# Transposed one-hots by a broadcast load, expansions between the steps of the scan chain, and one load of eight wait counts

## The reference

```python
ZU = einsum('nd,kdr->knr', Z, U)               # K = 4 heads of R = 16: 64 numbers per node
logits = (ZU[:, src] * ZU[:, dst]).sum(-1) / sqrt(R)
exp_l  = exp(logits - segment_max(logits, dst)[:, dst])
alpha  = exp_l / (segment_sum(exp_l, dst)[:, dst] + 1e-16)
agg    = segment_sum(alpha[..., None] * ZU[:, src], dst)
```

## Time and profile before

| | before |
|---|---|
| median of 3 runs | 3706.7 us |
| the profiled execution, its own time | 3677.74 us |
| its span (first to last instruction) | 3675.2 us |
| busy: PE, DVE, POOL, ACT | 54%, 52%, 47%, 32% |
| share of the 16 DMA engines: SP's queue, POOL's queue | 15.4%, 9.8% |
| granted TensorE clock, mean | 0.577 of full speed |

### The profile page before, as it was taken

One profiled execution on the slowest core, in us unless ns is written; L12 is line 12 of the kernel. 1 busy time (PEld: TensorE's weight loads), 2 busy tenths in 40 slices (PEclk: granted clock), 3 DMA queues, 4 the chain that ended last, 5 costly groups with the idle time before them and its releaser, 6 DMA issues. The chain is left out here.

```text
span 3675.2 us, 61713 instructions
## 1 busy us (share of the span) xinstructions
PE 1971.2 (54%) x15251; PEld 1490.8 (41%) x15252; DVE 1919.5 (52%) x5864; ACT 1168.6 (32%) x3040; POOL 1728.5 (47%) x1832
## 2 busy tenths in 40 slices
PE   9345545454545445454545455464545454567776
PEld 9233333343434334343424243343433333444666
DVE  4444646454545546454545455464545454666477
ACT  1112323222232323322232233233232322334477
POOL 1544454445444444554544544445544444252662
PEclk7555555555555555555555555555555555577798
DMA  6212222121212212121212112121212121285343
GB/s 205 52 32 46 47 44 46 42 46 42 48 41 47 46 41 48 42 49 40 47 39 48 42 44 48 41 50 41 48 40 45 41 49 39 58 274 179 112 140 107
DMA packets 406593, 232.96 MB, mean 63 GB/s; under 512 B 284096, under 2 KB 371434, under 8 KB 406506
## 3 DMA queue, kind: packets, MB, share of 16 engines
q1 hardware_dynamic: 346666, 154.11, 15.4%
q0 software_dynamic: 59840, 77.87, 9.8%
HBM read 134.80 MB, written 42.55 MB: 48 GB/s over the span
## 5 line engine op out<-in xcount | busy, mean ns | idle before, releaser
L576 POOL DMA_INDIRECT arena<-z_table,sslot x1563 | 1492.0, 955 | 1646.2 <-SPq L418 1114.0
L1347 PE MATMUL bank<-arena 128*128 x4992 | 613.8, 222 | 637.7 <-issue 585.8
L1347 PEld LDWEIGHTS bank<-arena 128*128 128x128 bf16 x4992 | 457.5, 105 | 789.5 <-issue 697.0
L1584 ACT ACTIVATE arena<-bank 128x272 f32<-128x272 f32 x416 | 269.8, 661 | 1574.8 <-remote 970.4
L902 DVE TENSOR_TENSOR xin<-arena,bank 128x512 f32<-128x512 f32 x208 | 143.1, 688 | 1044.3 <-remote 588.2
L1561 ACT ACTIVATE acc<-xTb 128x68 f32 x1600 | 384.6, 312 | 306.6 <-issue 296.0
L1364 PE MATMUL bank<-xto,arena 128*128 128x68 bf16 x3328 | 321.6, 246 | 147.5 <-issue 147.4
L1335 PE MATMUL bank<-ident_b,arena 128*128 128x128 bf16 x1664 | 214.8, 310 | 339.4 <-remote 205.3
L1364 PE MATMUL bank<-arena 128*128 128x68 bf16 x1664 | 296.9, 243 | 120.2 <-issue 90.5
L1364 PEld LDWEIGHTS bank<-xto,arena 128*128 128x128 bf16 x3328 | 281.5, 132 | 166.9 <-issue 166.9
L1335 PEld LDWEIGHTS bank<-ident_b,arena 128*128 128x128 bf16 x1664 | 160.4, 141 | 399.6 <-remote 200.2
(11 more groups left out here) (264 smaller groups left out, 2543.6 us busy)
## 6 DMA issues: line engine op xcount, KB each, us to landing
arena<-arena SPq DMA_DIRECT2D x1660, 32.0 KB
arena<-z_table,sslot POOLq DMA_INDIRECT x1563
dspace<-in_xT SPq DMA_DIRECT2D x49, 256.0 KB
xmz_table<-agn SPq DMA_DIRECT2D x49, 256.0 KB
xmz_table<-arena SPq DMA_DIRECT2D x14, 896.0 KB
arena<-in_x SPq DMA_DIRECT2D x13, 896.0 KB, 11.4
out<-arena SPq DMA_DIRECT2D x12, 896.0 KB
xin<-in_xT SPq DMA_DIRECT2D x8, 896.0 KB
```

The source lines that it names most:

```text
L576: pool.indirect_dma_start(ring[:, e % RING, :], None, z_table, bass.IndirectOffsetOnAxis(ap=sslot[:, e:e + 1], axis=0)).then_inc(tiles_in[ ...
L1347: last = T.matmul(zd_ps[g % 2][:, u * KR:(u + 1) * KR], onehotT[:, g * G + u, :], z3[:, bass.ds(tiles[u], 1), s, :].rearrange("p a c -> p ...
L1584: A.activation(sums[:, :, 1 + q * Q:1 + (q + 1) * Q].rearrange("p c j -> p j c"), sum_ps[q % 2][:, 0:Q * AW].rearrange("p (j c) -> p j c", ...
```

## The change

1. The transposed one-hots no longer come from PE and ACT. At the start VectorE writes `dloc` (for every step a row with its 128 edges' node numbers within the tile) as bf16 (`place`), SyncE stores it to a DRAM tensor `place_rows`, and for each block loads 32 of its rows, 8 KB, broadcast to all 128 partitions, into `onehotT` (`load_places`, a transfer that writes 1 MB). VectorE compares it in place with the partition's number (`make_onehotT`: `first_col` first, then four instructions of 128 x 1024 bf16), between its first scan and `copy_indices`.
2. The 32 transposes of a block, the waits around them, and ACT's four copies and `first_col` go.
3. `zd_ps` has four banks in place of two, one per group. PE expands groups 0, 1 and 2 of block b + 1 in the gaps of the chain of block b, where transposes 0, 1 and 2 were, and group 3 after the first half of `add_up`. `multiply_x` and `xmz` use bank 3.
4. SyncE loads a block's eight counts at once (`load_needs`, at the start of a turn) in place of two per group. `load_places(b + 1)` stands between the copies of groups 2 and 3, and waits until all expansions of block b are done.

```diff
+            def load_places(b):
+                if not (type(b) is int and b == 0):
+                    sp.wait_ge(zd_ready, NG * b)
+                    sp.nop(nofuse=True)
+                sp.dma_start(onehotT.rearrange("p j e -> p (j e)"),
+                             spread(place_rows[bass.ds(b * B, B), :].rearrange("(a j) e -> a (j e)", a=1), 0, P)).then_inc(places_in, 16)
...
+            def load_needs(b):
+                _, need = nc.values_load_multi_w_load_instructions(
+                    needs[0:1, bass.ds(b * NG * 2, 2 * NG)], engines=[mybir.EngineType.SP], min_val=16 * G, max_val=16 * G * EG)
+                return need
...
-                    need = [sp.value_load(needs[0:1, bass.ds((b * NG + g) * 2 + i, 1)], min_val=16 * G, max_val=16 * G * EG) for i in range(2)]
                     for i in range(2):
-                        sp.wait_ge(tiles_in[i], need[i])
+                        sp.wait_ge(tiles_in[i], need[2 * g + i])
...
-            def turn(b, h, uses, store, load):
+            def turn(b, h, uses, store, load, places=True):
+                need = load_needs(b)
                 for g in range(2):
-                    copy_steps(b, h, g, uses)
+                    copy_steps(b, h, g, uses, need)
                 sp.wait_ge(x_ready, b - 1)
+                sp.nop(nofuse=True)
                 load_resets(b, h)
...
-                for g in range(2, NG):
-                    copy_steps(b, h, g, uses)
+                copy_steps(b, h, 2, uses, need)
+                if places:
+                    load_places(b + 1)
+                copy_steps(b, h, 3, uses, need)
...
+            sp.wait_ge(places_out, 16)
+            sp.wait_ge(tab_read, 5)
+            load_places(0)
             sp.wait_ge(prep_read, 6)
             load_tiles(0, 0)
+            load_places(1)
...
+            def make_onehotT(b, h):
+                dve.wait_ge(places_in, 16 * (b + 1))
+                V.tensor_scalar(first_col[:, h:h + 1], onehotT[:, 0, 0:1], pno[:, 0:1], None, ALU.is_equal).then_inc(v_step, 1)
+                dve.wait_ge(v_step, vn.next())
+                for g in range(NG):
+                    part = onehotT[:, g * G:(g + 1) * G, :].rearrange("p j e -> p (j e)")
+                    V.tensor_scalar(part, part, pno[:, 0:1], None, ALU.is_equal).then_inc(oneT_ready, 1)
...
                 V.tensor_tensor_scan(fwd0, rs[:, 0:P], mid_ps[:, 0:P], NEG, ALU.add, ALU.max).then_inc(ends_ready, 1)
                 if more:
+                    make_onehotT(b + 1, 1 - h)
                     copy_indices(b + 1, 1 - h)
...
             def expand(b, g):
                 tiles = steps_of(b, g)
-                if g >= 2 or not (type(b) is int and b == 0):
-                    pe.wait_ge(zd_used, NG * b + g - 1)
+                if not (type(b) is int and b == 0):
+                    pe.wait_ge(zd_used, NG * (b - 1) + g + 1)
...
-                next_transposes(0)
+                if more:
+                    expand(b + 1, 0)
                 pe.wait_ge(carry_ready, b + 1)
...
-                next_transposes(1)
+                if more:
+                    expand(b + 1, 1)
                 pe.wait_ge(heads_ready, b + 1)
...
-                next_transposes(2)
+                if more:
+                    expand(b + 1, 2)
                 pe.wait_ge(back_ready, b + 1)
...
-                if more:
-                    expand(b + 1, 0)
-                    if dense:
-                        pe.wait_ge(xmz_copied, b)
-                    expand(b + 1, 1)
                 add_up(b, h, 0, 4)
                 if more:
-                    expand(b + 1, 2)
-                add_up(b, h, 4, 6)
-                if more:
+                    if dense:
+                        pe.wait_ge(xmz_copied, b)
                     expand(b + 1, 3)
-                add_up(b, h, 6, 8)
+                add_up(b, h, 4, 8)
```

More of the change, by code:

```diff
@@ L308, in program @@
         same = same_row.rearrange("p (c j) -> p c j", c=CH)
[L309 to L310 removed]
+        zd_ps = psum[2:6]
         mid_ps, row_ps = psum[6], psum[7]
@@ L767, in _ @@
             dve.wait_ge(v_step, vn.next())
+            dve.wait_ge(tab_ps, 1)
+            V.tensor_copy(place[:, :, :], dloc[:, :, :]).then_inc(place_ready, 1)
             V.memset(lastcol[:, 0:1], 0.0)
@@ L1326, in _ @@
             pe.wait_ge(prep_read, 6)
-            def transpose_onehots(b, h, g):
-                if g >= 2 or not (type(b) is int and b == 0):
-                    pe.wait_ge(oneT_ready, NG * b + g - 1)
-                pe.wait_ge(onehot_ready, NG * b + g + 1)
-                for u in range(G):
-                    last = T.transpose(tr_ps[g % 2][:, u * P:(u + 1) * P], onehot[:, h, g * G + u, :], ident_b[:, :])
-                last.then_inc(oneT_ps, 1)
             def expand(b, g):
                 tiles = steps_of(b, g)
-                if g >= 2 or not (type(b) is int and b == 0):
-                    pe.wait_ge(zd_used, NG * b + g - 1)
+                if not (type(b) is int and b == 0):
+                    pe.wait_ge(zd_used, NG * (b - 1) + g + 1)
                 pe.wait_ge(oneT_ready, NG * b + g + 1)
@@ L1562, in store_states @@
                                  ).then_inc(state_stored, 1)
-            def copy_onehots(b, h, g):
-                if not (type(b) is int and b == 0):
-                    act.wait_ge(zd_ready, NG * (b - 1) + g + 1)
-                act.wait_ge(oneT_ps, NG * b + g + 1)
-                if g == 0:
-                    A.activation(first_col[:, h:h + 1], tr_ps[0][:, 0:1], ACT.Copy)
-                A.activation(onehotT[:, g * G:(g + 1) * G, :].rearrange("p j e -> p (j e)"), tr_ps[g % 2][:, :], ACT.Copy).then_inc(oneT_ready, 1)
             def copy_keeps(b):
@@ L1616, in period @@
                         act.wait_ge(xmz_out, 16 * (b - 1))
-                    A.activation(xmz, zd_ps[1][:, :], ACT.Copy, bias=-ETA * LAM).then_inc(xmz_copied, 1)
+                    A.activation(xmz, zd_ps[NG - 1][:, :], ACT.Copy, bias=-ETA * LAM).then_inc(xmz_copied, 1)
                 copy_sums(b, first)
@@ L1624, in _ @@
             act.wait_ge(tab_read, 8)
-            for g in range(NG):
-                copy_onehots(0, 0, g)
             period(0, 0, dense=False)
```

52 lines of the change are left out of this document (22 added, 30 removed).

## The result

The changed kernel takes 3966.3 us (median of 4 runs, 3927.5 to 3977.7) where the kernel before, run beside it, takes 3705.4: a ratio of 1.068, 95% interval 1.060 to 1.0765. It is slower by 261 us where 80 us less were forecast, and lies above the range. The direction is that of the slower rival (a block of 65 us, 4010 us), which had a chance of 0.32.

A forecast was written before the change was run, and what follows sets the result against it. The prediction held that waits, not a busy engine, set the 59.1 us block, 26.3 us being two VectorE waits. 50 blocks x -1.8 us plus 8 at the start gave -82 us, so 3625 us; range 3420 to 3890.

The forecast's parts named there:

- slower rival: PE's queue between row of heads and last column: one more slow spell catches the chain; block 65, 4010 us; chance 0.32.
- One load of eight counts: SyncE's count loads: about 0.9 us less per group, cost 0, bounds -0.9 x 4 and +5 us a block.
- Four isolated bursts: POOL's gathers: more bursts of 8 and fewer of 16, the interval between groups staying near 12 us.
- Where the spells fall: PE's gaps in the chain: slow spells hit expansion 0 (+5.3 us) and expansion 2 (about +2), +7.3 us a block.
- Products of the last group: VectorE's last products start at T + 30.5, not T + 41.7, after SyncE's copies of group 3: -11.2 us a block.
- The compares: VectorE's path after the first scan: four compares of 0.45 us plus `first_col`, +2.1 us, between 1.3 and 3.7.
- Expansions stick out: PE's expansions 0 to 2 in the chain's gaps: the second and third stick out by 1.1 and 2.1, +3.2 us.
- 1 MB transfers: SyncE's broadcast loads: hidden, cost 0, upper bound 7 us; a rival had copies held up 2 us, 3706 us, chance 0.11.
- Gathers stalled by wide compares: POOL's gathers beside VectorE's compares: each compare adds its length to the burst, +94 us, 3720 us; chance 0.03.

The follow-up runs named there:

- e1: The kernel before, with SyncE loading a block's eight counts at once: 3935.0 us, ratio 1.065.
- e11: e1 with the two old count loads per group put back, their results unused: 3706.5 us, ratio 1.003.
- e2: The changed kernel with the counts loaded by group as before: 3795.2 us, ratio 1.016.
- e7: The kernel before with gathers from the fifth group on replaced by plain loads of the same size: 2444.1 us.
- e15: The changed kernel with gathers from the fifth group on replaced by plain loads of the same size: 2794.1 us.
- e17: The kernel before with GpSimd waiting after every four gathers until they have landed: 3260.9 us, ratio 0.887.
- e12: e2 with expansions out of the chain: 0 and 1 behind the shifted x product, 2 behind half, 3 behind three quarters of the sums: 3898.5 us, ratio 1.054.
- e9: The kernel before with GpSimd starting each burst of eight gathers only when the eight before have landed: 3941.9 us, ratio 1.057.
- e18: The kernel before with GpSimd pausing for landing only in the middle of each group of eight gathers: 3824.7 us, ratio 1.035.

## Why the prediction was wrong

- **The step that failed is "One load of eight counts: cost 0".** The prediction saw that the interval between groups must stay above a burst's 10 us, estimated about 12 for it, and took the bound of +5 us a block as unlikely. The runs: +5.6 us a block (e1), two idle loads take it back (e11), and in the changed kernel it is some 5 of the 6.8 per cent (e2). What I missed is that the copies either escape the spell or are drawn out by it: the 8 instructions saved per group took 1.3 us at full pace (median of 207; I had said 0.9) and 2.9 on the mean, and they decide between copies at 0.65 and at 1.4 us, and so whether the next signal meets a burst under way.
- **"Four isolated bursts"** was therefore wrong for the changed kernel (43 long ones) and right for e2 (13).
- **Where the spells fall**, +7.3 us, was under-sized even with short bursts. In e2 the stretch from rows to last column is 22.7 us against 13.8 before. I had put only the stretches of one block on a clock, with spells 1 to 2 us off the expansions; bursts drift against the chain. I had also left VectorE's queue out of the spells. The 5.9 us that VectorE stood before the last column in that block were not PE's: its product started at 1561.98 and VectorE took the column at 1569.17.
- **Products of the last group, -11.2 us**: first to last products fell by 9.7, ended by the copies' landing as foretold. The gain is real only where spells are: in e7 the products took 8.7 us and the change made them 1.7 longer.
- **The compares, +2.1 us**: measured +1.9 (four in 1.85 us, 0.46 each in a row and 0.49 singly; scan to rows 2.0 to 3.9). The Trainium skill's figure ("VectorE: DVE Perf Modes", section "The perf-mode tier table") gave 0.43 as an estimate, 7 to 12% under what the trace has.
- **Expansions stick out by 3.2 us**: 2.9 in e15, where no spell touches them. With the compares that is 4.7 of e15's 6.5.
- **1 MB transfers**: the copies behind them cost at most the 1.7 us of e15, and the compares wait for them 29.6 us in all.
- **Gathers stalled by wide compares**: as a price of 94 us that rival is out, since a gather takes 968 ns on the mean after and 955 before. The effect itself is there. The 57 gathers that ran beside a compare took 1.09 us each (the row at 2202.43 took 1.28), the other 1506 took 0.96; at the same place in the kernel before they take 0.95. In e15 the plain loads take 0.73 and 0.55 us. That is 57 x 0.13, some 7 us of GpSimd's time in all. The rule of the Trainium skill behind it ("SBUF — State Buffer", section "SBUF: two separate sides"), that GpSimd gets no descriptors written beside a two-port mode of VectorE, agrees with these rows in its direction.
- **The slower rival** had the stretch right (between the row of heads and the last column), PE's queue only for the smaller part of it, and its condition half right: what decided was not the start of expansion 2 but whether SyncE's signal falls inside a burst, which the rival named last ("if SyncE's shorter groups let two bursts merge"). It deserved the larger chance.

## What to carry to other kernels

Before moving work about, ask what slows everything at once. Here it was a run of indirect gathers: the fastest version that leaves nothing out adds two waits and removes nothing (e17, 11% under the kernel before). An instruction that nobody waits for still sets when a signal rises: saving 1.3 us per group cost 5.6 us per block. A wait is not the fault of the engine that makes what is waited for, unless its work ended late: compare the two times. And a mean over all instructions hides what a few of them pay, so split them by what ran beside them. To find out what a removed instruction was good for, put it back with its result unused. And test a reordering twice, as it is and with the disturbance taken out, because its sign can differ: the products of a block came 9.7 us closer together with the spells and 1.7 us further apart without them.

## What the runs showed of the hardware

- Indirect gathers by GpSimd of 128 rows each, one after another at 1.25 us, slow the starting of instructions on the other engines. In e1 TensorE started 38 matmuls in the third window and 3 in the fourth, with five gathers in each. In the kernel before, SyncE's copies go from 0.65 to 1.4 us apart, and ScalarE's stores of states stand 296 us for "issue" (8 us of idle time with plain loads). In e12 VectorE waits up to 6.8 us for its own copy. Four in a row show little of it ("issue" idle time of the expansions 77 us against 586), five more (160), eight a spell of about 6 us, sixteen one of about 17. Plain loads of the same rows' size from the same queue show none (slow share 0.6% against 36%).
- A pause until the gathers have landed, 2.2 us at the median, is enough after four gathers. It is not between eights (e9), nor once eights are among the fours (e18).
- Gathers beside a bf16 compare of 128 x 1024 on VectorE take GpSimd 1.09 us each and not 0.96.
- What in the chip the other engines lack during a spell, no run here shows. The mean load of the DMA engines it is not (share 0.15 in the spell of e1, 0.23 ahead of it).
- The clock is not the cause: TensorE's granted clock was 0.50, the level of 1.2 GHz, in the spell of e1 and in the window behind it alike, where it started 34 matmuls again.
